# Row sort as two lanes of neighbours, bias rows on all partitions, sixteen image stores, new instruction orders

## The chip, the cores and the metric

The kernel runs on one core of a Trainium2 chip. The metric is the device time of one execution in microseconds (us), as the median of several runs. TensorE is called PE here, VectorE DVE, ScalarE ACT, GpSimd POOL and SyncE SP, as in the profile. All of the arithmetic is float32 but for one mask matmul.

## What is computed

Eight images of 32 x 32 tokens with 128 channels go through a deformable convolution, a correlation layer that sorts, windowed attention, a mixture of experts, a state-space layer and a second mixture of experts. What the change touches is this:

```python
om = conv3x3(xn, om_kernel) + om_bias            # offsets and masks
cols = bilinear gather of xn at (base + offset), times mask
x1 = x + cols.reshape(B, OH, OW, 9 * C) @ kernel + bias
...
x3 = x.reshape(b, m, c)                          # m = 1024 tokens
corr = jnp.einsum('bmc,bnc->bmn', x3, x3) / c
x_sort = jnp.sort(corr, axis=-1)[..., ::-1]
ranks = jnp.round(jnp.linspace(1.0, m - 1, 128)).astype(jnp.int32)
return x_sort[..., ranks]
```

So every one of the 1024 rows of an image's correlation matrix, 1024 values long, is sorted in descending order, and 128 of its ranks are kept.

## The kernel before

**Units.** An image is two units (halves h = 0 and 1) of 512 tokens. A unit's rows lie as four tiles: 128 partitions, each with 4 rows of 1024 values, so 4096 values in a partition. The stages of the program are F (group norm, deformable convolution and correlation of the next image), S (the sort, on DVE alone), C (attention, first experts, state-space layer) and M (second experts). They are software pipelined: while image i is sorted, F works on image i + 1, C on the halves (i - 1, 1) and (i, 0), and M on image i - 1.

**What sets the order.** Each engine runs its instructions in program order. The generators of the stages are woven by strings of letters in the table `ORDER` (`weave`, near the end of the file): a letter says from which stage the next piece comes. There is a string for each engine and each kind of image: fill (F of image 0 alone), early (image 0), full (images 1 to 6), late (image 7) and drain. Engines are tied by semaphores alone. POOL has the gathers of F and nothing else.

**The sort.** `pe_corr` makes the sum and the absolute difference of two halves of the columns, so that PE and ACT do the first compare-exchange (larger and smaller of each pair); ACT writes both to `corr` (L695) through `there`. `dve_S` does the rest with TENSOR_TENSOR max and min. Before, the row is 8 places of 128 values; a network that sorts 8 works across the places (`exchange`, L808 and L810, and L818 to L834), and its last layer scatters the results so that each run of 8 lies together: `Y` is a view of `corr` in which neighbours of an instruction's output are 8 values (32 bytes) apart. Then odd-even merges make runs of 16, 32, ... 512 (`compare` L794 and L796; `pairs` L873, L881, L901, L903; `eighth` L893; copies of the ends of runs L877 and L880), each down to distance k = 1. A bitonic merge of the two runs of 512 follows, of which the last steps (L927) make the wanted ranks alone. `corr` is free for the next unit (`corr_used`) after the compare of m = 16. Max and min of one step are two instructions; `link` is a semaphore that DVE counts for its own results.

**The image store.** `sp_F` writes the normalized image `xn_tok` four times, shifted, to `quads` in DRAM, so that one gather of 2 KB brings the four neighbours of a point: 8 token tiles x 4 corners = 32 stores of 64 KB an image, each with the outermost dimension ROWS = 4 in the destination. POOL gathers (`pool_F`) after all of the stores and after `idx` (L722), which DVE makes from the offsets. SP also issues the loads of the experts' weights (`e1w`, `e2w`), in the order that its strings give.

**Bias rows.** `conv_bias`, `bo_row` and `cb_row` lie on one partition and are added by a matmul with a row of ones (L605, L1053, L1296).

## Time and profile before

| | |
|---|---|
| median of 3 runs | 4914.16 us (4904.60 to 4914.23) |
| profiled execution | 4910.64 us, span 4908.8 us |
| DVE busy | 4267.6 us, 87% of the span |
| PE busy | 3958.7 us, 81% |
| ACT busy | 2954.4 us, 60% |
| POOL busy | 884.1 us, 18% |

The profile is of one execution. Its span goes from the first instruction to the last, and its own time is 1.8 us above the span. A busy share is a mean over fill, eight images and drain, which have different limits; a row of a group of instructions gives their count, summed busy time and the mean of one in ns, and behind the second bar the idle time of the engine just before them.

### The profile page before, as it was taken

What the parts mean: (1) busy time and instruction counts of PE and PEld (TensorE: products, weight loads), DVE (VectorE), ACT (ScalarE), POOL (GpSimd) and SP (SyncE); (2) the same over time, 40 slices, a digit from 0 to 9 for tenths busy, and PEclk for the clock granted to TensorE, in tenths of its full rate; (3) what the DMA queues carried; (4) which work ended last, traced back from release to release, by engine and by line L of the source; (5) the groups of instructions that cost most, each with busy time, mean ns of one, the idle gap of its engine ahead of it and who ended that gap; (6) DMA issues with size and microseconds to landing.
All of it is one profiled execution on the core that took longest, in us unless ns stands there. A gap on an engine that the chain in (4) does not pass through costs nothing.

```text
span 4908.8 us, 56286 instructions
## 1 busy us (share of the span) xinstructions
PE 3958.7 (81%) x19410; PEld 2667.5 (54%) x19410; DVE 4267.6 (87%) x5380; ACT 2954.4 (60%) x7241; POOL 884.1 (18%) x580
## 2 busy tenths in 40 slices
PE   5747748889798988989798988989798987867587
PEld 3616424567456654567456654567456654545354
DVE  1098999999999999999999999999999999999521
ACT  4526526687467846687467846677467845554452
POOL 2316000242005300242005300242005300000000
PEclk8878869999799998999799988999799998988798
DMA  4314100232013210232013210232013210010001
GB/s 132 98 35 123 37 0 18 67 105 63 16 43 110 79 36 18 71 104 65 11 43 110 79 36 18 71 102 63 14 44 110 77 34 16 20 30 27 10 24 37
DMA packets 226037, 269.28 MB, mean 55 GB/s; under 512 B 26831, under 2 KB 188506, under 8 KB 225626
## 3 DMA queue, kind: packets, MB, share of 16 engines
q0 software_dynamic: 46080, 151.03, 10.6%
q1 hardware_dynamic: 179674, 114.65, 8.0%
q8 instruction: 156, 2.56, 0.2%
q14 instruction: 127, 1.04, 0.1%
HBM read 242.25 MB, written 23.34 MB: 54 GB/s over the span
## 4 chain that ended last, share of the span: by engine, by line
DVE 41%; PE 36%; ACT 9%; issue 6%; POOL 4%; DMA 4%; SPq 1%; DVEq 0%; POOLq 0%; ACTq 0%
PE bank L597 5%; POOL gath L759 4%; PE bank L1298 3%; PE bank L1633 3%; PE bank L1628 3%; DMA gath<-quads,idx 3%; PE bank L1613 3%; DVE srt_b L794 3%; DVE srt_b L881 3%; DVE srt_b L796 3%; DVE srt_a L893 2%; DVE srt_b L873 2%; DVE srt_a L794 2%; DVE srt_a L796 2%; PE bank L569 2%
## 5 line engine op out<-in xcount | busy, mean ns | idle before, releaser
L759 POOL DMA_INDIRECT gath<-quads,idx x576 | 883.9, 1535 | 3075.4 <-DVE idx L722 1990.3
L597 PE MATMUL bank<-diag,gath 128*128 128x128 f32 x4608 | 615.0, 296 | 168.5 <-DMA gath<-quads,idx 168.5
L639 ACT ACTIVATE diag<-ident,w 128x128 f32<-128x128 f32 x2304 | 704.7, 393 | 30.7 <-DVE w L737 21.2
L597 PEld LDWEIGHTS bank<-diag,gath 128*128 128x128 f32 x4608 | 593.8, 211 | 203.9 <-DMA gath<-quads,idx 187.6
L1613 PEld LDWEIGHTS bank<-e2w,act 128*128 128x128 f32 (+1 forms) x3072 | 408.0, 198 | 161.3 <-issue 156.7
L1628 PE MATMUL bank<-mu_t,e2w 128*128 128x512 f32 (+1 forms) x768 | 421.9, 632 | 82.4 <-DMA e2w<-moe_w_t 36.2
L1633 PE MATMUL bank<-gated_u,e2w 128*128 128x512 f32 (+1 forms) x768 | 426.2, 638 | 36.7 <-DVE act L1713 32.9
L1713 DVE TENSOR_TENSOR act<-act,bank 128x512 f32<-128x512 f32 (+1 forms) x384 | 261.0, 680 | 183.6 <-PE bank L1633 160.8
L1613 PE MATMUL bank<-e2w,act 128*128 128x128 f32 (+1 forms) x3072 | 413.2, 281 | 1.6 <-DVE act L1713 1.6
L1681 ACT ACTIVATE act<-bank 128x512 f32<-128x512 f32 (+1 forms) x384 | 227.6, 593 | 208.6 <-PE bank L1628 206.0
L873 DVE TENSOR_TENSOR srt_b<-srt_a 128x1024 f32<-128x1024 f32 x192 | 350.9, 1828 | 1.5 <-issue 0.3
L881 DVE TENSOR_TENSOR srt_b<-srt_a 128x1024 f32<-128x1024 f32 x192 | 351.1, 1829 | 0.0
L1681 ACT ACT_TABLE_LOAD x199 | 255.3, 1283 | 3.4 <-PE bank L1613 0.4
L672 ACT ACTIVATE cols<-bank 128x384 f32<-128x384 f32 x192 | 93.0, 484 | 241.6 <-PE bank L597 235.8
L1633 PEld LDWEIGHTS bank<-gated_u,e2w 128*128 128x128 f32 (+1 forms) x768 | 131.3, 187 | 189.3 <-issue 166.6
L794 DVE TENSOR_TENSOR srt_b<-srt_a 128x2048 f32<-128x2048 f32 x96 | 219.3, 2285 | 1.4
L794 DVE TENSOR_TENSOR srt_a<-srt_b 128x2048 f32<-128x2048 f32 x96 | 219.2, 2283 | 0.9
L796 DVE TENSOR_TENSOR srt_b<-srt_a 128x2048 f32<-128x2048 f32 x96 | 219.2, 2283 | 0.0
L796 DVE TENSOR_TENSOR srt_a<-srt_b 128x2048 f32<-128x2048 f32 x96 | 219.1, 2283 | 0.0
L901 DVE TENSOR_TENSOR srt_a<-srt_b 128x2016 f32<-128x2016 f32 (+1 forms) x96 | 211.5, 2203 | 0.9
L903 DVE TENSOR_TENSOR srt_a<-srt_b 128x2016 f32<-128x2016 f32 (+1 forms) x96 | 211.6, 2204 | 0.0
L1628 PEld LDWEIGHTS bank<-mu_t,e2w 128*128 128x128 f32 (+1 forms) x768 | 121.3, 186 | 145.0 <-issue 73.5
(348 smaller groups left out, 8134.4 us busy)
## 6 DMA issues: line engine op xcount, KB each, us to landing
e2w<-moe_w_t SPq DMA_DIRECT2D x256, 170.5 KB
quads<-xn_tok SPq DMA_DIRECT2D x256, 64.0 KB
e1w<-L_ffn_w SPq DMA_DIRECT2D x256, 64.0 KB, 1.9
e2w<-moe_w_t SPq DMA_DIRECT2D x256, 64.0 KB
gath<-quads,idx POOLq DMA_INDIRECT x576
e2w<-moe_w_t SPq DMA_DIRECT2D x128, 42.5 KB
x_tok<-x SPq DMA_DIRECT2D x8, 512.0 KB, 4.4
out<-tm SPq DMA_DIRECT2D x16, 256.0 KB, 2.5
```

Source lines behind the costliest of these rows:

```text
L597: ins = T.matmul(FB[q % 2][:, k * P:(k + 1) * P], gath[:, g % 2, k, s * C:(s + 1) * C], diag[:, g % 2, 4 * k + s], start=(s == 0), stop=(s ...
L639: ins = SC.activation(diag[:, g % 2, n], ident[:], ACT.Copy, scale=w[:, n:n + 1])
L759: pool.indirect_dma_start(gath[:, g % 2, k], None, quads, bass.IndirectOffsetOnAxis(idx[:, TG * g + k:TG * g + k + 1], 0)).then_inc(sem["g ...
L794: V.tensor_tensor(dst[:, :, 0:size // 2], lo, hi, ALU.max)
L796: return V.tensor_tensor(dst[:, :, size // 2:size], lo, hi, ALU.min)
L873: V.tensor_tensor(out_lo, lo, hi, ALU.max)
L881: link.put(V.tensor_tensor(out_hi, lo, hi, ALU.min))
L1613: ins = T.matmul(MB[2][:, t * P:(t + 1) * P], act2[0:m, n % ACT2_SLOTS, t * P:(t + 1) * P], e2w[0:m, e % 2, W2 + k * C:W2 + (k + 1) * C], ...
L1628: T.matmul(MB[r % 2][0:m, :], e2w[:, e % 2, k * P:k * P + m], mu_t[:], start=True, stop=True).then_inc(sem["m_ps"], 1)
L1633: T.matmul(MB[r % 2][0:m, :], e2w[:, e % 2, W3 + k * P:W3 + k * P + m], gated_u[:], start=True, stop=True).then_inc(sem["m_ps"], 1)
L1681: SC.activation(act2[0:m, n % ACT2_SLOTS], MB[r % 2][0:m, :], ACT.Silu).then_inc(sem["m_sb"], 1)
L1713: V.tensor_tensor(act2[0:m, n % ACT2_SLOTS], act2[0:m, n % ACT2_SLOTS], MB[r % 2][0:m, :], ALU.mult).then_inc(sem["hh"], 1)
```

## The change

1. **Sort.** The pair that PE and ACT compare is now token j with token j + 512 (`sd` from the two contiguous halves of `yn_t`), and ACT writes the results in groups of four values: two larger, two smaller (`w=2`). A row is so two interleaved lanes of 512 values, and every later instruction moves at least two neighbours together. The network of 8 is gone. Odd-even merges run from m = 8 to m = 1024 and stop at distance k = 2, after which each lane is sorted. A new step compares lane 0 with lane 1 reversed and writes two halves apart (L876 and L878 of the new file), in place of the compare of size 1024. The rest of the bitonic merge is as it was. `corr` is only read, and is released after the first two instructions of a unit.
2. **Stores.** 16 stores of 128 KB take the place of 32 of 64 KB. Each takes 32 partitions of `xn_tok` with all eight tiles, and has the outermost dimension x = 32. They begin when both halves of `xn_tok` are there.
3. **Bias rows** are loaded to all 128 partitions and added by a matmul with the identity. In the preparation one DVE instruction and a wider matmul are added for it.
4. **Orders.** All strings but those of the fill and SP_early are new.

```diff
-        "CCCMMMCCCCCCCCMMFFMMMMMMMMCMCCCMCMMMF"
+        "CCCMMFFCMCCCCMCCCMMMMMMMMMCCCCMCMFMMM"
...
-        conv_bias = sb("conv_bias", [1, C])
+        conv_bias = sb("conv_bias", [P, C])
...
-            load(conv_bias[:], A["L0_conv_bias"].rearrange("a b c f -> (a b c) f"))
+            load(conv_bias[:], A["L0_conv_bias"].rearrange("a b c f -> (a b c f)").partition_broadcast(P))
...
+            V.tensor_scalar(tc[:, 1], ones[:], bqk[:, 2:3], None, ALU.mult)
...
-            T.matmul(CB[0][0:1, 0:C], bqk[:, 2:3], wqkvo[:, 3], start=True, stop=True).then_inc(prep, 1)
+            T.matmul(CB[0][:, 0:C], tc[:, 1], wqkvo[:, 3], start=True, stop=True).then_inc(prep, 1)
...
-            for t in range(NT):
-                if t % 4 == 0:
-                    sp.wait_ge(sem["xn_tok"], img("xn_tok", i, t // 4 + 1))
-                    settle(sp)
-                if t == 0:
-                    sp.wait_ge(sem["gath0"], img("gath0", i, 0))
-                    settle(sp)
-                    sp.wait_ge(sem["gath1"], img("gath1", i, 0))
-                    settle(sp)
-                for dy in range(2):
-                    for dx in range(2):
-                        there = q[ROWS * t + 1 - dy:ROWS * t + 1 - dy + ROWS, 1 - dx:1 - dx + WIDTH, 2 * dy + dx]
-                        sp.dma_start(there, xn_tok[:, t]).then_inc(sem["quad_out"], 16)
-                if t % 4 == 3:
-                    yield
+            sp.wait_ge(sem["xn_tok"], img("xn_tok", i, 2))
+            settle(sp)
+            sp.wait_ge(sem["gath0"], img("gath0", i, 0))
+            settle(sp)
+            sp.wait_ge(sem["gath1"], img("gath1", i, 0))
+            settle(sp)
+            for dy in range(2):
+                for dx in range(2):
+                    for r in range(ROWS):
+                        there = q[r + 1 - dy:r + 2 - dy + HEIGHT - ROWS:ROWS, 1 - dx:1 - dx + WIDTH, 2 * dy + dx]
+                        sp.dma_start(there.rearrange("t x c -> x t c"),
+                                     xn_tok[WIDTH * r:WIDTH * (r + 1)]).then_inc(sem["quad_out"], 16)
+                yield
...
-                    T.matmul(out, ones[0:1, :], conv_bias[:], start=False, stop=False)
+                    T.matmul(out, ident[:], conv_bias[:], start=False, stop=False)
...
-                there = corr[:, t % UT].rearrange("p (s k r) -> p s k r", k=2, r=P)
+                there = corr[:, t % UT].rearrange("p (b k w) -> p b k w", k=2, w=2)
...
-                    SC.activation(there[:, :, k], FB[1 - k][:].rearrange("p (s r) -> p s r", r=P), ACT.Identity,
+                    SC.activation(there[:, :, k], FB[1 - k][:].rearrange("p (b w) -> p b w", w=2), ACT.Identity,
...
-            pairs = yn_t[:].rearrange("p (s k r) -> p s k r", k=2, r=P)
-            V.tensor_tensor(sd[:, 1], pairs[:, :, 0], pairs[:, :, 1], ALU.subtract)
-            V.tensor_tensor(sd[:, 0], pairs[:, :, 0], pairs[:, :, 1], ALU.add).then_inc(sem["sd"], 1)
+            V.tensor_tensor(sd[:, 1], yn_t[:, 0:HALF], yn_t[:, HALF:TOK], ALU.subtract)
+            V.tensor_tensor(sd[:, 0], yn_t[:, 0:HALF], yn_t[:, HALF:TOK], ALU.add).then_inc(sem["sd"], 1)
...
-                if size == TOK:
-                    hi = hi[:, :, ::-1]
...
-            def places(buf):
-                return buf[:].rearrange("p g (s r) -> p g s r", s=8)
-
-            X, L, R, Y = places(corr), places(srt_a), places(srt_b), corr[:].rearrange("p g (r s) -> p g s r", s=8)
-
-            def exchange(lo, hi, out_lo, out_hi):
-
-                V.tensor_tensor(out_lo, lo, hi, ALU.max)
-                yield
-                link.put(V.tensor_tensor(out_hi, lo, hi, ALU.min))
-                yield
-                link.wait()
-
-            def fours(buf, b):
-                return buf.rearrange("p g (a b c) r -> p g a b (c r)", a=2, b=2)[:, :, :, b]
-
-            yield from exchange(fours(X, 0), fours(X, 1), fours(R, 0), fours(R, 1))
-            V.tensor_tensor(X[:, :, 1::4], R[:, :, 1::4], R[:, :, 2::4], ALU.max)
-            yield
-            link.put(V.tensor_tensor(X[:, :, 2::4], R[:, :, 1::4], R[:, :, 2::4], ALU.min))
-            yield
-            V.tensor_tensor(L[:, :, 3], R[:, :, 3], R[:, :, 7], ALU.max)
-            link.wait()
-            V.tensor_tensor(R[:, :, 1], X[:, :, 1], X[:, :, 5], ALU.max)
-            yield
-            V.tensor_tensor(L[:, :, 2], X[:, :, 2], X[:, :, 6], ALU.max)
-            V.tensor_tensor(L[:, :, 5], X[:, :, 1], X[:, :, 5], ALU.min)
-            yield
-            link.put(V.tensor_tensor(R[:, :, 6], X[:, :, 2], X[:, :, 6], ALU.min))
-            V.tensor_tensor(L[:, :, 4], R[:, :, 0], R[:, :, 4], ALU.min)
-            yield
-            link.wait()
-            V.tensor_tensor(Y[:, :, 0], R[:, :, 0], R[:, :, 4], ALU.max)
-            link.put(V.tensor_tensor(Y[:, :, 7], R[:, :, 3], R[:, :, 7], ALU.min))
-            yield
-            link.wait()
-            yield from exchange(L[:, :, 2:4], L[:, :, 4:6], R[:, :, 2:4], R[:, :, 4:6])
-            yield from exchange(R[:, :, 1:7:2], R[:, :, 2:7:2], Y[:, :, 1:7:2], Y[:, :, 2:7:2])
-            now = 1
-            m = 16
-            while m < TOK:
-                first = m == 16
-                if not first:
+            ins = yield from compare(8, runs(corr, 8), runs(srt_a, 8))
+            ins.then_inc(sem["corr_used"], 1)
+            yield
+            dve.wait_ge(sem["corr_used"], unit("corr_used", i, h))
+            now = 0
+            m = 8
+            while m <= TOK:
+                if m > 8:
                     link.wait()
-                ins = yield from compare(m, runs(corr if first else bufs[now], m), runs(bufs[1 - now], m))
-                if first:
-                    ins.then_inc(sem["corr_used"], 1)
-                else:
+                    ins = yield from compare(m, runs(bufs[now], m), runs(bufs[1 - now], m))
                     link.put(ins)
-                yield
-                if first:
-                    dve.wait_ge(sem["corr_used"], unit("corr_used", i, h))
-                now = 1 - now
+                    yield
+                    now = 1 - now
                 here, there = runs(bufs[now], m), runs(bufs[1 - now], m)
 
...
-                while k >= 1:
+                while k >= 2:
                     lo, hi = pairs(here, k)
                     out_lo, out_hi = pairs(there, k)
                     link.wait()
                     V.tensor_tensor(out_lo, lo, hi, ALU.max)
                     yield
-                    if k == 1:
-
-                        V.tensor_copy(edges(there, 0, 1), edges(here, 0, 1))
+                    if m == 8:
+
+                        link.put(V.tensor_tensor(hi, lo, hi, ALU.min))
+                        yield
+                        link.wait()
+                        link.put(V.tensor_copy(lo, out_lo))
+                        yield
+                        break
+                    if k == 2:
+
+                        V.tensor_copy(edges(there, 0, 2), edges(here, 0, 2))
                     elif k < m // 4:
 
                         V.tensor_copy(edges(there, 1, k // 2), edges(here, 1, k // 2))
                     link.put(V.tensor_tensor(out_hi, lo, hi, ALU.min))
                     yield
-                    if k == 1:
+                    if k == 2:
...
-            k = TOK
+            pair = bufs[now][:].rearrange("p g (j w) -> p g j w", w=2)
+            lo, hi = pair[:, :, :, 0], pair[:, :, ::-1, 1]
+            half = bufs[1 - now][:].rearrange("p g (w j) -> p g w j", w=2)
+            link.wait()
+            V.tensor_tensor(half[:, :, 0], lo, hi, ALU.max)
+            yield
+            link.put(V.tensor_tensor(half[:, :, 1], lo, hi, ALU.min))
+            yield
+            now = 1 - now
+            k = TOK // 2
```

Three places in the orders. On DVE, the start of the sort of image 1 (full), before; `srt_b` and `srt_a` are the sort's two buffers, the other rows belong to C and M:

```order
L808 TENSOR_TENSOR srt_b<-corr 128x8x256
L810 TENSOR_TENSOR srt_b<-corr 128x8x256
L1073 RECIPROCAL lnsd<-lnsd 128x4
L1074 SCALAR_TENSOR_TENSOR nmr<-lnmv,lnsd 128x4
L818 TENSOR_TENSOR corr<-srt_b 128x8x128
L820 TENSOR_TENSOR corr<-srt_b 128x8x128
L1152 TENSOR_REDUCE msm<-bank 128x4
L1153 TENSOR_TENSOR ml<-bank,msm 128x32
L822 TENSOR_TENSOR srt_a<-srt_b 128x4x128
L824 TENSOR_TENSOR srt_b<-corr 128x4x128
L826 TENSOR_TENSOR srt_a<-corr 128x4x128
L827 TENSOR_TENSOR srt_a<-corr 128x4x128
```

DVE at the same place now:

```order
L790 TENSOR_TENSOR srt_a<-corr 128x512x4
L792 TENSOR_TENSOR srt_a<-corr 128x512x4
L1046 RECIPROCAL lnsd<-lnsd 128x4
L1047 SCALAR_TENSOR_TENSOR nmr<-lnmv,lnsd 128x4
L829 TENSOR_TENSOR srt_b<-srt_a 128x512x2
L833 TENSOR_TENSOR srt_a<-srt_a 128x512x2
L836 COPY srt_a<-srt_b 128x512x2
L790 TENSOR_TENSOR srt_b<-srt_a 128x256x8
L792 TENSOR_TENSOR srt_b<-srt_a 128x256x8
L1125 TENSOR_REDUCE msm<-bank 128x4
L1126 TENSOR_TENSOR ml<-bank,msm 128x32
L829 TENSOR_TENSOR srt_a<-srt_b 128x256x4
```

The sixteen instructions of the 8-network begin here with two over 8 x 256 values, and in their place stand the compare of m = 8 and its one odd-even step with a copy; pieces are 4 or 2 values long every 8.

On SP, in the first full image, the loads of the second experts (`e2w`) and the stores of the next image, before:

```order
L1566 DMA e2w<-moe_w_t 128x341
L1568 DMA e2w<-moe_w_t 128x128 x2
L1568 DMA e2w<-moe_w_t 85x128
L502 DMA quads<-xn_tok 4x32x128 x32
L1565 DMA e2w<-moe_w_t 128x341
L1566 DMA e2w<-moe_w_t 128x341
L1568 DMA e2w<-moe_w_t 128x128 x2
L1568 DMA e2w<-moe_w_t 85x128
L1565 DMA e2w<-moe_w_t 128x341
```

SP at the stores of the same image now, with loads of the first experts (`e1w`) behind them:

```order
L1541 DMA e2w<-moe_w_t 85x128
L1538 DMA e2w<-moe_w_t 128x341
L1539 DMA e2w<-moe_w_t 128x341
L1541 DMA e2w<-moe_w_t 128x128 x2
L1541 DMA e2w<-moe_w_t 85x128
L501 DMA quads<-xn_tok 32x8x128 x16
L962 DMA e1w<-L_ffn_w 128x128
L963 DMA e1w<-L_ffn_w 128x128
L1538 DMA e2w<-moe_w_t 128x341
L1539 DMA e2w<-moe_w_t 128x341
L1541 DMA e2w<-moe_w_t 128x128 x2
L1541 DMA e2w<-moe_w_t 85x128
```

The stores now stand after the second set of `e2w` loads of the image, where before they followed the fifth, and eight pairs of `e1w` loads (lines 989 and 990 before, 962 and 963 now) that stood ahead of them stand behind.

On PE, in the same image, the transposes of the next image's normalized tokens, after which ACT makes `xn_tok`, before:

```order
L1633 MATMUL bank<-gated_u,e2w 128x512
L1312 MATMUL bank<-arena 128x128 x4
L1613 MATMUL bank<-e2w,act 128x128 x4
L1628 MATMUL bank<-mu_t,e2w 128x512
L1633 MATMUL bank<-gated_u,e2w 128x512
L1613 MATMUL bank<-e2w,act 128x128 x4
L561 MATMUL bank<-ident,yn_t 128x128 x4
L1628 MATMUL bank<-mu_t,e2w 85x512
L561 MATMUL bank<-ident,yn_t 128x128 x4
L1633 MATMUL bank<-gated_u,e2w 85x512
L1613 MATMUL bank<-e2w,act 128x128 x4
L1604 MATMUL bank<-gate_diag,mu 128x128 x4
```

PE at the transposes of the same image now (L952 and L1179 belong to the first experts of C):

```order
L1586 MATMUL bank<-e2w,act 128x128 x4
L1601 MATMUL bank<-mu_t,e2w 128x512
L1606 MATMUL bank<-gated_u,e2w 128x512
L1586 MATMUL bank<-e2w,act 128x128 x4
L1601 MATMUL bank<-mu_t,e2w 85x512
L560 MATMUL bank<-ident,yn_t 128x128 x8
L952 MATMUL bank<-ident,gates 8x128 x4
L1606 MATMUL bank<-gated_u,e2w 85x512
L1586 MATMUL bank<-e2w,act 128x128 x4
L1179 MATMUL bank<-u_t,e1w 128x512
L1183 MATMUL bank<-b,arena 128x128 x4
L1577 MATMUL bank<-gate_diag,mu 128x128 x4
```

The transposes (`bank<-ident,yn_t`) stand 59 rows earlier in PE's order, just ahead of the matmuls of a half's first experts (L1179), where before they followed a state-space layer's projections.

## Rows read from the trace of the kernel before

**Rows 1.** Page: busy us (share) xinstructions by engine; the chain by engine.

```profile
PE 3958.7 (81%) x19410; PEld 2667.5 (54%) x19410; DVE 4267.6 (87%) x5380; ACT 2954.4 (60%) x7241; POOL 884.1 (18%) x580
...
DVE 41%; PE 36%; ACT 9%; issue 6%; POOL 4%; DMA 4%; SPq 1%; DVEq 0%; POOLq 0%; ACTq 0%
```

**Rows 2.** Stretches: length, busy us and count by engine, PE clock, DMA share, GB/s.

```profile
0.00:247.70 247.70, 156.22 (x871) 121.63 (x871) 16.46 (x47) 118.92 (x356) 68.37 (x76) 0.88 0.39 114
...
2943.00:3496.00 553.00, 484.55 (x2427) 328.60 (x2426) 531.27 (x670) 369.53 (x907) 117.31 (x72) 0.92 0.20 60
...
4048.00:4586.00 538.00, 368.68 (x1554) 228.67 (x1554) 520.60 (x626) 260.51 (x556) 0.00 (x0) 0.84 0.07 21
4586.00:4908.80 322.80, 257.80 (x1126) 162.20 (x1126) 77.95 (x214) 161.86 (x346) 0.00 (x0) 0.89 0.09 27
```

**Rows 3.** Waits of DVE in one full image (2943 to 3496 us): us, times, longest.

```profile
DVE dtx L1476 <- ACT dtr L1404: 5.6, 2, 3.9
DVE act L1713 <- PE bank L1633: 4.4, 4, 2.2
DVE act L1713 <- ACT act L1681: 2.4, 2, 2.1
```

**Rows 4.** Groups by line and shape, DVE: count, busy us, mean ns, idle before.

```profile
L810 DVE TENSOR_TENSOR corr<-srt_b 128x1536 f32<-128x1536 f32 x16 | 47.1, 2942 | 0.0
...
L794 DVE TENSOR_TENSOR srt_a<-corr 128x2048 f32<-128x2048 f32 x16 | 36.5, 2284 | 0.0
...
L820 DVE TENSOR_TENSOR corr<-srt_b 128x1024 f32<-128x1024 f32 x16 | 19.5, 1218 | 0.0
...
L903 DVE TENSOR_TENSOR srt_a<-srt_b 128x2040 f32<-128x2040 f32 x16 | 36.4, 2276 | 0.0
...
L834 DVE TENSOR_TENSOR corr<-srt_b 128x512 f32<-128x512 f32 x16 | 17.6, 1099 | 0.0
...
L822 DVE TENSOR_TENSOR srt_a<-srt_b 128x512 f32<-128x512 f32 x16 | 10.9, 682 | 0.0
...
L877 DVE COPY srt_b<-srt_a 128x512 f32<-128x512 f32 x16 | 10.4, 648 | 0.0
L880 DVE COPY srt_a<-srt_b 128x256 f32<-128x256 f32 x32 | 9.3, 291 | 0.0
...
L880 DVE COPY srt_b<-srt_a 128x64 f32<-128x64 f32 x32 | 6.0, 189 | 0.0
```

**Rows 5.** DVE in order of time, first unit: start us, us of two instructions together.

```profile
275.15 1.29 DVE L893 TENSOR_TENSOR srt_a<-srt_a,srt_b 128x512 f32<-128x512 f32 x2
```

**Rows 6.** All engines in order of time, fill: start us, us, instruction.

```profile
34.94 22.66 SPq L502 DMA_DIRECT2D quads<-xn_tok  x32
...
55.49 0.23 DVE L722 SCALAR_TENSOR_TENSOR idx<-cols 128x72 uint32<-128x72 f32 x1
...
57.54 7.12 ACT L639 ACTIVATE diag<-ident,w 128x128 f32<-128x128 f32 x24 [4.04 <-DVE w L737]
62.10 1.08 POOL L759 DMA_INDIRECT gath<-quads,idx  x1 [61.66 <-DMA quads<-xn_tok]
...
68.51 3.79 PE L597 MATMUL bank<-diag,gath 128*128 128x128 f32 x16 [15.52 <-DMA gath<-quads,idx]
```

**Rows 7.** DMA while SP stores `quads`: the same columns as rows 2.

```profile
318.00:334.00 16.00, 13.36 (x38) 3.50 (x36) 15.86 (x10) 3.06 (x5) 0.00 (x0) 1.00 0.29 86
```

**Rows 8.** DMA view of 2310 to 2320 us, 40 slices: one store of `out` in it.

```profile
GB/s 0 0 0 0 0 0 0 0 0 0 0 0 0 0 0 59 293 287 295 115 0 0 0 0 0 0 33 0 0 0 0 0 0 0 0 0 0 0 0 0
```

**Rows 9.** Before the sort of image 2: start us, us; last `corr` written, first read.

```profile
1282.44 0.60 ACT L695 ACTIVATE corr<-bank 128x512 f32<-128x512 f32 x1 [1.12 <-PE bank L630]
...
1287.69 2.29 DVE L808 TENSOR_TENSOR srt_b<-corr 128x2048 f32<-128x2048 f32 x1
```

**Rows 10.** Groups by line and shape, PE: two matmuls of 320 columns.

```profile
L1298 PE MATMUL bank<-w_xbc,u_t 128*128 128x320 f32 x512 | 169.3, 478 | 0.0
...
L1296 PE MATMUL bank<-cb_row,ones 1*128 1x320 f32 x128 | 55.8, 517 | 0.0
```

More of the change, by code:

```diff
@@ L1052, in pe_att @@
             T.matmul(CB[0][:], ident[:], flat(u), start=False, stop=False)
-            T.matmul(CB[0][:], ones[0:1, :], row4(bo_row[:]), start=False, stop=False)
+            T.matmul(CB[0][:], ident[:], row4(bo_row[:]), start=False, stop=False)
             yield
@@ L1295, in pe_ssm @@
                 if conv:
-                    T.matmul(out[:, 0:XBC], ones[0:1, :], cb_row[:], start=True, stop=False)
+                    T.matmul(out[:, 0:XBC], ident[:], cb_row[:], start=True, stop=False)
                     for k in range(CONVK):
```

100 lines of the change are left out of this document (50 added, 50 removed).

## The prediction

> **What bounds the kernel now.** I read the page first: DVE is busy 87% of the span and leads the chain of work that ended last, with PE behind it [rows 1]. A mean hides the stages, so the table of stretches comes next [rows 2]. In the fill (to 247.7 us) DVE does nearly nothing and PE, ACT and the gathers set the time. In a full image, 2943 to 3496 us standing for six alike, DVE works 531.3 of 553.0 us, PE 484.6 and ACT 369.5. In the late image DVE works 520.6 of 538.0. Only in the drain, the last 322.8 us, is DVE idle again and PE the busiest. So from 247.7 to 4586 us the time is DVE's work plus some 22 us of idleness an image. The list of its waits shows many short ones on ACT and PE, the longest 3.9 us [rows 3]. What is taken from DVE's work here should come off the end almost whole; what is taken from PE or ACT should not.
>
> **The sort, per unit.** Contiguous max and min fit a line: 512 values 682 ns, 1024 values 1218, 2048 values 2284 [rows 4], so 1.043 ns a value and 148 ns fixed. Two of 512 stand in 1.29 us together [rows 5], so each starts 0.08 us before the other is recorded as done and the fixed part on the path is about 0.07 us. Removed are the network, 16 instructions over 15360 values (4096 + 2048 + 3072 + 1024 + 2048 + 3072), and the six steps of distance 1 in m = 16 to 512, 12 instructions over 2 x 11784 = 23568 values. Added are m = 8, 4 instructions over 6144 values, and m = 1024, 22 instructions over 32784. Both sums are 38928 values: the comparisons are the same, in 26 instructions instead of 28, which is 0.14 us. The gain lies elsewhere. The last network layer writes single values 32 bytes apart: 1536 values in 2942 ns, where the line gives 1750, and 512 values in 1099 ns, where contiguous ones take 682 [rows 4]. Two of each are 2 x 1.19 + 2 x 0.42 = 3.2 us, and all of it goes. Copies cost something back. Three copies of ends at distance 1 go: 0.65 us for the 512 values of m = 16, and by its rate and the shorter rows 0.29 and 0.19 for 128 and 32. New are 1024 values in pairs, and ends of 256, 64 and 16. Copies in pieces give 291 ns for 256 and 189 for 64 [rows 4], 0.53 ns a value: 0.70 us for 1024, and 0.66 for the three. That is 1.36 against 1.13, a loss of 0.23. Net 3.2 + 0.14 - 0.23 = 3.1 us a unit, **50 us in 16 units**.
>
> Patterns that are new have these bounds. The pieces of 4 and 2 values every 8 (7168 values a unit): nearest is the step on eighths of a run at m = 16, pieces of 8 bytes every 64, two in 1.29 us with nothing on top [rows 5]; the far end is the 0.8 ns a value of the scattered write. I take nothing, since the pieces are alike. The merge across lanes reads every second value, one side backwards: the distance-1 step over 2040 values reads and writes every second one in 2276 ns, on the line [rows 4], so I take nothing. The copy of 1024 could go at the rate of 648 ns for 512 single values, 0.4 us a unit or 6 us in all more. The rows show that single values every 32 bytes pay and every 8 bytes don't. The Trainium skill, SBUF — State Buffer, section on the DMA port swizzle, says that accesses run at full bandwidth when at least two in a row hit the same 16-byte line. By that rule all new patterns are free, on ACT's side too, and the sum stays; by the far end it would be the slower rival below.
>
> ACT writes `corr` in pieces of 8 bytes every 16 instead of blocks. The eviction takes 0.60 us [rows 9], eight of them for a half; even doubled they add 4.8 us to a chain that ACT, with 180 us free an image, otherwise bears.
>
> **The corr chain** is the cover to watch. The last `corr` of image 2 is written at 1282.44 + 0.60 = 1283.0 us and DVE first reads it at 1287.7 [rows 9]: 4.7 us of cover. DVE gains 6.2 us an image, so with F where it was, DVE would wait 1.5 us at each of seven image starts, 10 us in all. In the new order the transposes stand 59 rows earlier on PE, and `corr` is released after two instructions instead of after the compare of m = 16, so I take nothing and keep the 10 us for the range.
>
> **Stores.** In the fill SP issues 32 stores from 34.94 us for 22.66 us, and POOL's first gather waits for them until 62.10 [rows 6]. While they run, the DMA engines are busy to 0.29 and move 86 GB/s [rows 7], where the store of `out`, outermost dimension 128, reaches 290 GB/s with shares of 9 tenths [rows 8]. So a store with outermost dimension 4 uses about 4 of 16 engines. With 32 outermost, 2 MB would take 7.2 us at 290 GB/s; at the old issue time of 22.66 / 32 = 0.71 us each, 16 take 11.3. From 35 us on they have landed by 51 us even with the 4.5 us of the old tail. The gathers also need `idx`, which DVE writes at 55.49 + 0.23 us [rows 6]; so POOL starts near 55.9, 6.2 us sooner, and not 15. ACT's first weights (from 57.54, 12 in 3.6 us) and PE's first gather matmul (68.51) follow at 61 to 62.5 us. Against this stand one DVE instruction in the preparation and 288 KB of broadcast loads, 1.0 us at 290 GB/s if nothing hides them: 0.8 us. The fill gives **5.4 us**. In later images the stores lie beside DVE's sort and give SP 10 us or more.
>
> A rule speaks against the new stores. The Trainium skill, SBUF — State Buffer, section on the DMA port swizzle, says that 32 partitions reach only 8 of 16 ports, 189 GB/s as measured there. By it the stores would take 11 us instead of 7; `idx` still comes later, so the sum stays.
>
> **Bias rows.** The matmul with one row of ones over 320 columns takes 517 ns, that with 128 rows 478 [rows 10]. The rows don't set the time, and PE is not the bound: nothing.
>
> **Orders.** They move waits and no work. DVE's 22 us an image are spread over many short waits [rows 3], and what the new strings make of them no row can show. Bounds: a better order could halve them, 7 x 10 = 70 us less; a worse one adds as much. I take no change, because PE keeps 68 us free an image [rows 2].
>
> **Sum.** 4908.8 - 50 - 5.4 = 4853.4 us of span, 4855.2 with the 1.8 us around it. The profiled execution (4910.64) is 3.5 us under the median of the runs, which I leave out: **4855 us**, 1.2% less.
>
> **Rivals.**
> - Better orders: DVE's waits fall by 10 us in most images, 4855 - 60 = 4795. For it: the longest waits are 2 to 4 us in the image shown, and sit on few places. Against: the order before already left few. 15%.
> - Waits grow: DVE is faster, PE and ACT are not, and the chains that release DVE come late, by the 1.5 us above or up to 4 us an image. 4865 to 4900, say 4882. 22%.
> - The change doesn't gain: 50 us of new waits eat the sort's gain, 4905 to 4923. PE's 68 us free would have to lie in the wrong places. 4%.
> - Slower: pieces of 4 and 2 values every 8 pay like single ones. 7168 x 0.78 ns = 5.6 us a unit, 89 us in 16, so 4944. It decides from 3.1 us / 7168 = 0.43 ns a value. The eighths at m = 16 speak against it [rows 5]. 4%.
> - Slower by SP: the stores stand three `e2w` sets and eight `e1w` pairs earlier, and SP holds everything behind them until both halves of `xn_tok` are there. If PE reaches the transposes late, experts' weights come late, and PE, then DVE, wait. It decides from the point at which PE's 68 us are used up; 15 us an image more would give 4855 + 105 = 4960. The transposes moved along on PE, which speaks against it. 5%.
>
> **Chances.** My forecast (4840 to 4865) 50%, the rest as above. The range leaves out the two slower cases, the one without gain and the tip of the better orders: 4795 to 4897 us. A measurement of this kernel can tell about 0.2% (10 us) from no change. Faster by more 0.87, within it 0.04, slower 0.09.
>
> **What would show it.** DVE's busy time down by about 50 us with 15 fewer instructions; the first two instructions of a unit at 2284 ns and the step at m = 8 at 1218; the copy of 1024 near 700 ns; the sort's lane merge at 2284. The stretch of a full image near 547 us with 22 us idle. In the fill, 16 stores over 7 to 11 us with a DMA share well over 0.3, POOL's first gather at 56 us waiting for `idx`, and the first sort at 242 us. A wait for `corr` at the start of a unit would show the cover gone; a wait of PE for `e1w` or `e2w` the SP rival. A new eviction time over 0.6 us on ACT would show that its pieces cost.

## The result and the profile after

| | before | changed |
|---|---|---|
| median | 4910.75 us (4904.6 to 4914.23) | **4749.86 us** (4744.98 to 4753.61) |
| profiled execution | 4910.64 us, span 4908.8 | 4753.48 us, span 4751.4 |
| mean granted TensorE clock, of 2.4 GHz | 0.896 | 0.909 |

The ratio is 0.9676, with a 95% interval of 0.9664 to 0.9688. The change takes off 161 us, 3.3%. The forecast was 55 us, and the time lies 45 us below its range.

The page of the changed kernel, to be held against [rows 1]: busy time by engine, and the shares of the chain that ended last.

```profile
PE 3878.9 (82%) x19410; PEld 2642.8 (56%) x19410; DVE 4219.8 (89%) x5365; ACT 3009.5 (63%) x7284; POOL 928.2 (20%) x580
...
DVE 74%; PE 15%; issue 6%; ACT 3%; DMA 1%; SPq 1%; POOL 0%; DVEq 0%; POOLq 0%; ACTq 0%
```

DVE's busy time is 48 us less. PE's is 80 us less with the same 19410 instructions, which the forecast didn't foresee. The chain now runs over DVE for 74% of the span instead of 41%, and over PE for 15% instead of 36%.

Stretches of the changed kernel: length, busy us by engine (PE, PEld, DVE, ACT, POOL), PE clock, DMA share, GB/s. They are the fill, the first image, a full image, the late image and the drain.

```profile
0.00:241.30 241.30, 153.69 (x870) 120.35 (x870) 16.73 (x47) 119.52 (x356) 68.39 (x76) 0.88 0.42 118
241.30:710.10 468.80, 280.77 (x1305) 198.95 (x1306) 460.38 (x475) 198.84 (x551) 125.19 (x72) 0.78 0.18 51
...
2840.20:3371.50 531.30, 466.46 (x2427) 318.93 (x2426) 524.96 (x670) 376.97 (x913) 122.37 (x72) 0.95 0.21 62
3905.10:4426.90 521.80, 375.85 (x1554) 235.31 (x1552) 514.27 (x619) 262.92 (x557) 0.00 (x0) 0.84 0.07 22
4426.90:4751.40 324.50, 259.78 (x1126) 166.91 (x1126) 78.46 (x214) 167.00 (x350) 0.00 (x0) 0.86 0.09 27
```

By stage the time went as follows (first unit's sort to first unit's sort; full images are the mean of six):

| us | before | changed | less |
|---|---|---|---|
| fill | 247.7 | 241.3 | 6.4 |
| first image | 489.1 | 468.8 | 20.3 |
| a full image | 551.9 | 532.5 | 19.4, and 117 in six |
| late image | 537.9 | 521.9 | 16.0 |
| drain | 322.5 | 324.4 | -1.9 |

In a full image DVE's work fell from 531.3 us [rows 2] to 525.0 in the row shown, the 6.2 us of the forecast. The other 13 us are idle time: DVE had 20 to 22 us of it an image, and has 6 to 8.5 now. That is the term that was missed. The waits of DVE over all stages with a sort show it (us in total, times, longest). First the kernel before:

```profile
DVE dtx L1476 <- ACT dtr L1404: 34.9, 15, 3.9
DVE act L1713 <- PE bank L1633: 30.0, 19, 4.9
...
DVE lnsd L1073 <- ACT lnsd L1063: 14.6, 1, 14.6
DVE arena L1539 <- PE bank L1361: 12.4, 9, 1.5
DVE act L1713 <- ACT act L1681: 11.2, 12, 2.1
```

and the changed one:

```profile
DVE arena L1512 <- PE bank L1334: 8.6, 8, 1.7
DVE lnsd L1046 <- issue: 3.2, 1, 3.2
DVE act L1686 <- PE bank L1606: 1.3, 2, 0.9
```

The 35 us for `dtr`, the 41 for `act` and 11 of the 15 for `lnsd` are gone or all but gone. What is left idle in an image is mostly the spacing between instructions.

### The profile page after: what moved, and what is told of

It reads as the page before. It is cut to its first block, busy times and chain, and to the rows that moved or that the text cites. A ratio compares the mean times of both kernels' runs of the same rounds, so it can differ in the third digit from the quotient of the medians.

```text
span 4751.4 us, 56186 instructions
## 1 busy us (share of the span) xinstructions
PE 3878.9 (82%) x19410; PEld 2642.8 (56%) x19410; DVE 4219.8 (89%) x5365; ACT 3009.5 (63%) x7284; POOL 928.2 (20%) x580
## 3 DMA queue, kind: packets, MB, share of 16 engines
q14 instruction: 125, 1.02, 0.1%
## 4 chain that ended last, share of the span: by engine, by line
DVE 74%; PE 15%; issue 6%; ACT 3%; DMA 1%; SPq 1%; POOL 0%; DVEq 0%; POOLq 0%; ACTq 0%
DVE srt_b L845 6%; DVE srt_b L829 6%; DVE srt_a L792 5%; DVE srt_a L790 5%; DVE srt_a L857 4%; DVE srt_b L792 4%; DVE act L1686 4%; DVE srt_a L867 4%; DVE srt_a L845 4%; DVE srt_b L790 4%; DVE srt_a L865 3%; DVE srt_b L857 3%; DVE srt_a L829 3%; PE bank L596 2%; DVE srt_b L865 2%
## 5 line engine op out<-in xcount | busy, mean ns | idle before, releaser
L757 POOL DMA_INDIRECT gath<-quads,idx x576 | 928.0, 1611 | 2844.1 <-DVE idx L721 1861.2
L596 PE MATMUL bank<-diag,gath 128*128 128x128 f32 x4608 | 598.1, 291 | 134.4 <-DMA gath<-quads,idx 127.2
L596 PEld LDWEIGHTS bank<-diag,gath 128*128 128x128 f32 x4608 | 579.7, 206 | 173.6 <-DMA gath<-quads,idx 145.6
L1606 PE MATMUL bank<-gated_u,e2w 128*128 128x512 f32 (+1 forms) x768 | 440.2, 657 | 97.6 <-DVE act L1686 72.8
L1586 PEld LDWEIGHTS bank<-e2w,act 128*128 128x128 f32 (+1 forms) x3072 | 424.2, 204 | 165.4 <-issue 162.7
L1586 PE MATMUL bank<-e2w,act 128*128 128x128 f32 (+1 forms) x3072 | 428.8, 288 | 0.8 <-DVE act L1686 0.6
L829 DVE TENSOR_TENSOR srt_b<-srt_a 128x1024 f32<-128x1024 f32 (+3 forms) x208 | 370.1, 1779 | 2.3 <-issue 0.2
L845 DVE TENSOR_TENSOR srt_b<-srt_a 128x1024 f32<-128x1024 f32 x192 | 350.6, 1826 | 0.0
L790 DVE TENSOR_TENSOR srt_a<-srt_b 128x2048 f32<-128x2048 f32 x112 | 255.8, 2284 | 0.8
L792 DVE TENSOR_TENSOR srt_a<-srt_b 128x2048 f32<-128x2048 f32 x112 | 255.8, 2284 | 0.0
L792 DVE TENSOR_TENSOR srt_b<-srt_a 128x2048 f32<-128x2048 f32 x96 | 219.3, 2284 | 0.0
L829 DVE TENSOR_TENSOR srt_a<-srt_b 128x1024 f32<-128x1024 f32 (+2 forms) x112 | 194.3, 1735 | 1.5
```

Source lines behind the costliest of these rows:

```text
L596: ins = T.matmul(FB[q % 2][:, k * P:(k + 1) * P], gath[:, g % 2, k, s * C:(s + 1) * C], diag[:, g % 2, 4 * k + s], start=(s == 0), stop=(s ...
L757: pool.indirect_dma_start(gath[:, g % 2, k], None, quads, bass.IndirectOffsetOnAxis(idx[:, TG * g + k:TG * g + k + 1], 0)).then_inc(sem["g ...
L790: V.tensor_tensor(dst[:, :, 0:size // 2], lo, hi, ALU.max)
L792: return V.tensor_tensor(dst[:, :, size // 2:size], lo, hi, ALU.min)
L829: V.tensor_tensor(out_lo, lo, hi, ALU.max)
L845: link.put(V.tensor_tensor(out_hi, lo, hi, ALU.min))
```

## Experiments: the parts one by one

First the parts were tried apart. Orders were exchanged over the new sort alone; the new orders without the new sort weren't tried. The edits are the hunks of the change, put in or left out:

```
sort    dve_S, sd and corr as changed; orders, stores and bias rows as before
stores  sp_F with 16 stores (quad_out 16 * 16); the rest as before
bias    conv_bias, bo_row, cb_row on [P, ...], ident[:] in place of ones[0:1, :]
orders  the ORDER table of the one kernel or of the other
```

> The kernel before with the new sort and its layout of corr alone; old strings, stores and bias rows. Theory 1: 16 x 3.1 = 50 us less, 4860 us. Theory 2 in its corr half: waits fall too, 4780 or lower. A third reading (DVE 6 us an image faster runs into chains that PE and ACT set): 4870 to 4890, with a wait for corr at the start of units.

> The kernel before with the 16 new stores alone. Theory 1: the fill 6 us shorter and nothing else, 4905 us. Theory 2 in its store half (expert loads that stood behind 22 us of stores were what PE and then DVE waited for): 10 us or more less in each of 7 images, 4840 or lower.

> The changed kernel with every order string of the kernel before; sort, stores and bias rows are new. Theory 1 (the new strings alone took DVE's waits of 14 us an image): 4855 us, DVE busy as in the changed kernel (4220), idle 22 us in a full image. Theory 2 (the early release of corr and the faster stores freed the chains that DVE waited for, whatever the strings): 4750 to 4780, idle about 8 us in a full image.

> The changed kernel with the 32 old stores, which now stand early in SP's strings. Theory 1: the fill 6 us longer, 4756 us. If the new strings lean on short stores (loads of e1w and e2w stand right behind them): waits of PE for e2w or e1w in each full image and 4775 to 4850 us.

These four left some 50 us without an owner: the sort alone took off 0.59%, the stores 0.18%, yet sort, stores and bias rows together 1.77%. So the bias rows, forecast at nothing, came under suspicion, and five more kernels completed the picture.

> The kernel before with the bias rows on 128 partitions and nothing else of the change. Theory A (the bias rows hold TensorE for 56 us): 4850 to 4885 us, and TensorE busy 473 us in a full image where 482 stood. Theory B (TensorE has slack of 60 us an image, so nothing shows): 4900 to 4910 us. In both the spacing at the bias rows falls to 1.30, 0.56 and 1.51 us.

> The kernel before with the new sort and correlation layout and the bias rows on 128 partitions; old orders, old 32 stores. The sort alone gave 4879, sort, bias rows and new stores together 4820. Theory A (bias rows): 4825 to 4840 us, with VectorE's idle time in a full image down from 20 to 26 us to 14 to 18. Theory B (what is missing comes from the sort and the short stores together): 4870 to 4880 us.

> The kernel before with the new sort and the 16 new stores; old orders, bias rows on one partition. Theory A (bias rows): the sum of sort and stores, 4865 to 4875 us. Theory B (sort and short stores together make up what neither gives alone): 4820 to 4830 us.

> The changed kernel with the bias rows back on one partition (rows of one partition against a row of ones), all else as changed. Theory A (the bias rows): in the traces the first output step after a one-partition bias matmul starts late, 1.69 us from the product before the conv bias row to the second product behind it against 1.30 us with the full-height bias, 0.94 against 0.56 at the 3x3 bias, 1.90 against 1.51 at the attention bias: 0.39 us each, 64 + 64 + 16 of them in the program, 56 us of TensorE's time, of which the chains that VectorE waits for take most. It expects 4785 to 4810 us, TensorE busy 476 us or more in a full image (468 in the changed kernel) and VectorE's idle time in one at 10 to 14 us instead of 7. Theory B (the orders alone hold the gain beyond the sort): 4745 to 4760 us and VectorE's idle time unchanged. Theory C (the new orders fit only the changed work): 4810 us or more, as with the old stores.

> The kernel before with the new sort and correlation layout and the new orders; old 32 stores, bias rows on one partition. The last corner of the cube of orders, stores and bias rows over the new sort. With the old orders it took 4879 us. If the parts add under the new orders (bias rows 32 us, stores 64 us over the changed kernel's 4750) it takes 4840 to 4855 us. If the new orders bring a gain of their own and both lacks fall into the same waits, 4815 to 4835 us. If the new orders need the other parts, 4870 us or more.

Measured, as ratios to the kernel before run beside them, with their 95% intervals:

| new parts | old orders | new orders |
|---|---|---|
| stores alone | 0.9982 (0.9972 to 0.9991), 4897.7 us | |
| bias alone | 0.9919 (0.9902 to 0.9935), 4863.0 us | |
| sort | 0.9941 (0.9925 to 0.9958), 4879.5 us | 0.9909 (0.9891 to 0.9927), 4853.5 us |
| sort, stores | 0.9945 (0.9929 to 0.9962), 4875.6 us | 0.9746 (0.9727 to 0.9766), 4781.8 us |
| sort, bias | 0.9839 (0.9822 to 0.9855), 4824.5 us | 0.9807 (0.9791 to 0.9824), 4814.2 us |
| sort, bias, stores | 0.9823 (0.9807 to 0.984), 4820.3 us | 0.9676 (0.9664 to 0.9688), 4749.9 us |

From one set of runs to the next the median of the kernel before moved between 4901 and 4911 us, so the ratios are compared; 0.01% is 0.49 us. The four runs of sort and stores under the new orders spread most, 4775 to 4800 us.

Of the first four expectations, the one for the sort alone was met in its third range (4870 to 4890), but with no wait for `corr` beyond the first sort's. The stores alone fell between their two theories (4897.7 us, and 3.5 us of the fill instead of 6), and so did the old orders (4820.3 us). The old stores met the second, with a wait for `e1w` in each full image. Of the next five, the bias rows alone lie in the range of theory A and the other three within 3.5 us of it, far from B; sort and orders alone lie where the parts add. Three things follow.

The **sort** alone is worth 29 us, over half of the 50 us that leave DVE: its idle time in a full image grew to 20 to 26 us. The **bias rows** are worth 40 us alone and, over the sort, 50 to 60 with the old orders and 34 to 50 with the new. The **orders** are worth 16 us as long as the old stores stand, with or without bias rows, and 72 to 98 us with the short ones. The stores in turn gave 9 us at most under the old orders, and 64 to 80 under the new. Orders and stores are one term, not two.

What the new orders take away is seen in the kernel that differs from the changed one in its orders alone, by DVE's waits over the same stages:

```profile
DVE act L1686 <- PE bank L1606: 26.6, 19, 3.9
...
DVE lnsd L1046 <- issue: 14.9, 1, 14.9
...
DVE dtx L1449 <- ACT dtr L1377: 9.8, 8, 2.5
DVE act L1686 <- ACT act L1654: 6.8, 5, 2.1
DVE msm L1125 <- PE bank L1558: 6.3, 4, 1.7
```

These are 64 us, of which 4.5 are left in the changed kernel, and its full images take 540.9 us instead of 532.5. Which of the strings does it was not tried: but for the last two stages they were exchanged all at once. The granted clock in a full image is also a little higher with them, 0.94 to 0.95 against 0.93 to 0.94, and whether that is a cause of the shorter time or follows from it, no run separates. Beside the bias rows it is no rival: with them alone it stayed at 0.93 to 0.94, where the kernel before had 0.92 to 0.93.

## Experiments: what the bias rows cost

The rows of PE's weight loads in order of time tell it, in the kernel before (start us, us, instruction; in brackets the idle time ahead and its cause):

```profile
2511.13 0.46 PEld L1300 LDWEIGHTS bank<-w_zdt,u_t 128*128 128x128 f32 x2
2511.93 0.29 PEld L1296 LDWEIGHTS bank<-cb_row,ones 1*128 1x128 f32 x2 [0.34 <-issue]
2512.66 1.91 PEld L1298 LDWEIGHTS bank<-w_xbc,u_t 128*128 128x128 f32 x8 [0.44 <-issue]
```

The load of the one-partition weights starts 0.34 us after the load ahead of it has ended, and the full one behind it 0.44 us after. Neither waits for a semaphore ("issue"). In the changed kernel such rows show no gap worth a bracket (medians 0.03 and 0.08 us):

```profile
2437.49 0.41 PEld L1269 LDWEIGHTS bank<-cb_row,ident 128*128 128x128 f32 x2
2437.99 2.07 PEld L1271 LDWEIGHTS bank<-w_xbc,u_t 128*128 128x128 f32 x8
```

The gaps are not the loss itself: at this place the two grow by 0.67 us together, and PE loses 0.39. That is read from start to start on PE, where each float32 product stands as two instructions. Around `cb_row` the five steps are 0.316, 0.374, 0.358, 0.373 and 0.269 us with the old row, and 0.222 and four times 0.269 with the new one: each of four steps is about 0.1 us longer. From the start of the instruction ahead of the bias row's two to the start of the third behind them:

| us | one partition | 128 partitions |
|---|---|---|
| `cb_row`, 64 times | 1.689 | 1.299 |
| `conv_bias`, 64 times | 0.943 | 0.558 |
| `bo_row`, 16 times | 1.898 | 1.508 |

These are medians, the same to 1 ns in four kernels with old rows and four with new ones. It is 0.39 us each time, 144 times, so **56 us of PE**. The means that the forecast compared, 517 and 478 ns [rows 10], hold a fifth of that (0.04 us for each of the two instructions), since the rest lies in the gaps and in the products behind.

Why DVE's time follows is seen in the kernel with the bias rows alone. Its waits of DVE, as above:

```profile
DVE act L1714 <- PE bank L1634: 31.9, 24, 5.0
DVE srt_b L809 <- ACT corr L696: 23.5, 1, 23.5
DVE lnsd L1074 <- issue: 21.0, 1, 21.0
DVE arena L1540 <- PE bank L1362: 10.6, 9, 1.7
DVE msm L1153 <- PE bank L1586: 10.1, 6, 2.1
DVE dtx L1477 <- ACT dtr L1405: 6.2, 8, 1.2
DVE act L1714 <- ACT act L1682: 3.2, 4, 1.4
```

DVE's wait for `dtr` falls from 34.9 us to 6.2, and that for ACT's part of `act` from 11.2 to 3.2: 37 us, of which 6 come back at `lnsd` and 4 at `msm`. `dtr` is made by ACT from the four products with `w_zdt`, and on PE these alternate with the convs that `cb_row` opens, so three convs stand ahead of the last. PE as a whole had 68 us free in an image, but at this place DVE was waiting. (The 24 us for `corr` are the first sort's wait, in every kernel.)

How low may the rows be? One kernel gave the bias matmuls of the changed kernel other heights:

```
-T.matmul(out[:, 0:XBC], ident[:], cb_row[:], ...
+T.matmul(out[:, 0:XBC], ident[0:64, :], cb_row[0:64], ...
...
-T.matmul(out, ident[:], conv_bias[:], ...
+T.matmul(out, ident[0:32, :], conv_bias[0:32], ...
...
-T.matmul(CB[0][:], ident[:], row4(bo_row[:]), ...
+T.matmul(CB[0][:], ident[0:96, :], row4(bo_row[:])[0:96], ...
```

> The changed kernel with each bias matmul on fewer partitions: the conv bias row on 64, the 3x3 bias on 32, the attention bias on 96 (the bias then reaches only that many rows of its tile, so this part of the computation is left out for the others). Read is the spacing of the products around each bias matmul. Theory A (any height under 128 breaks the overlap of weight load and product): 1.69, 0.94 and 1.90 us at all three, as with one partition, and about 4780 us. Theory B (only the narrowest rows do): 1.30, 0.56 and 1.51 us, and 4745 to 4755 us.

The spacing was 1.691 us at 64 partitions, 0.943 at 32 and 1.512 at 96, the time 4762.1 us (ratio 0.972, 0.9699 to 0.974). So both theories failed in part: 64 and 32 rows cost as much as one, 96 cost nothing. The kernel lost 12 us by its median and 22 by the ratio, less than the 32 to 34 of the kernel with all three rows on one partition, though 128 of the 144 places are as slow; that isn't explained. (It is two runs here, and four there that spread over 25 us.)

The matmuls of the second experts (L1586) narrow the step further. Some stand on 85 partitions among full ones, and their starts lie 0.112 us apart on both sides, as those of full ones do; one over 32 partitions behind them starts at 0.205 us. So the step lies between 64 and 85 partitions.

The Trainium skill has the rule behind this: TensorEngine Tiling (Array Packing), section Tiling Modes, lists 128, 64 and 32 rows as modes of the array and says that "Changing tiling mode (not just tile) drains the TensorE". The rows agree in where the step lies: 1, 32 and 64 partitions fit a smaller mode and pay, 85 and 96 need the full one and don't. That it is a drain, no row shows. Counted over PE's records, neighbours pass between at most 64 partitions and more 480 times in the kernel before and 192 times in the changed one; the edit takes away 144 changes there and back. Those left are at products over 8, 27 and 32 partitions. At 0.39 us there and back they would hold 37 us of PE, by an estimate; whether DVE waits for any of it, no run tells.

## Experiments: what the long stores cost under the new orders

With the 32 old stores under the new orders, DVE's largest wait and PE's wait for a load were, over all stages with a sort (us, times, longest):

```profile
DVE act L1688 <- PE bank L1608: 67.2, 14, 11.3
```

```profile
PE bank L1181 <- DMA e1w<-L_ffn_w: 52.2, 6, 9.2
```

PE waits once an image for a load of `e1w`, 9 us, and DVE as long for a product behind it; the changed kernel has 1.3 us of the one and none of the other. Nine of the ten us that a full image is longer (542.7 to 532.5) are these. SP's order in a full image is why: it stands in `CCCMMFFCM` at the stores (`FF`), waits 95 us for `xn_tok`, issues the stores, and only then the load of `e1w` that PE needs next. In the changed kernel the stores take 8.6 us, that load goes out at 2919.4, 9.4 us after the first store, and PE starts on it at 2927.4 without a wait. With the old stores it goes out 22.6 us after the first store, at 2972.7, and PE starts on it at 2976.8 after 8.6 us of idleness. The rival of the forecast had this mechanism; it was right about the place and wrong that the new kernel would suffer from it, because the stores got shorter.

To tell it from the traffic of the stores, they were moved six places down the string, behind five pairs of `e1w` and one set of `e2w` (the expectation counts one pair fewer, and its 128-byte rows are rows of 128 values):

```
-"CCCMMFFCMCCCCMCCCMMMM...
+"CCCMMCMCCCCFFMCCCMMMM...
```

> The changed kernel with the 32 old stores (4814 us), but in a full image with the stores five loads later in SyncE's order, behind four pairs of e1w and one load of e2w, which then no longer stand behind 22 us of stores. Theory A (the 10 us an image are the loads of e1w queued behind the stores: the profile has TensorE waiting 8.6 us once an image for e1w and VectorE 9.7 us for the product behind it): 4750 to 4775 us, and that wait is gone. Theory B (the traffic of the 128-byte-row stores itself or the later gather costs): 4805 us or more.

4824.3 us (0.9844, 0.9826 to 0.9861): nothing won, and in the range of theory B. Theory A seemed to fall, but the wait had moved. PE over all stages with a sort:

```profile
PE bank L1603 <- DMA e2w<-moe_w_t: 76.5, 15, 10.5
```

The wait for `e1w` is gone, and in its place PE waits 76.5 us for `e2w`, whose load now stands behind the stores; with the stores at the earlier place it was 14.8 us in 9 waits, 3.3 at most. DVE's wait for the product behind is 73.8 us. So the two halves of the stores went where no load behind them was due:

```
-"CCCMMFFCMCCCCMCCCMMMM...
+"CCCMMCMCCCCFMCCCFMMMM...
```

> The changed kernel with the 32 old stores (4814 us), in a full image in two halves of 11 us at two places of SyncE's order where no load behind them is due: one before the e2w load that goes out 11 us after the last paced pair of e1w, one behind the three unpaced pairs of e1w, where the next e2w load stood 16 us off. Theory A (what the long stores cost is the one load behind them that TensorE is next to want, whichever it is): 4755 to 4780 us, with no wait of TensorE for e1w or e2w over 3 us in a full image and VectorE's idle time there at 6 to 10 us. Theory B (long stores cost by their traffic or by the later gathers wherever they stand): 4805 to 4830 us, as in the two places tried.

**4751.5 us** (0.9676, 0.9653 to 0.9698) with the 32 old stores, the changed kernel's time. Full images take 531 to 533.5 us. What was 67.2 us of waiting is now:

```profile
DVE act L1688 <- PE bank L1608: 1.6, 2, 1.2
```

PE's waits for `e2w` are back at 15.4 us, 3.2 at most, against 15.7 and 3.5 in the changed kernel. Theory A holds, and the time is 3.5 us below its range: the cost was the one load next in line. So in full images the 16 stores bring nothing that a better place for the 32 doesn't. What they bring by themselves is 3.6 us of the fill (244.9 and 241.3 us).

## Experiments: the price of DVE's time, and the last stages

To price DVE's time, work of no use was added behind the sort's first two instructions:

```
...
+            V.tensor_reduce(more[:, 0:CONVK], w_xbc[:], AX.X, ALU.max)
+            V.tensor_reduce(more[:, CONVK:CONVK + TAPS], conv_w[:], AX.X, ALU.max)
...
```

> The changed kernel with two maxima over constants added behind the sort's first stage, 2432 elements in two instructions; by the 1153 ns of such an instruction over 960 elements that is 2.9 us a unit, 47 us in 16 units, their result unused. It prices VectorE's time under the new orders. Theory A (VectorE sets the time one to one, as the prediction had it): 4790 to 4800 us. Theory B (part of it fills idle time, 7 us an image): 4765 to 4785 us. Theory C (every us lengthens other waits too): over 4805 us.

The added instructions (busy us in all, mean ns):

```profile
L802 DVE TENSOR_REDUCE more<-w_xbc 128x4 f32<-128x1280 f32 x16 | 23.6, 1475 | 0.0
...
L803 DVE TENSOR_REDUCE more<-conv_w 128x9 f32<-128x1152 f32 x16 | 21.5, 1343 | 0.0
```

45.1 us of DVE's work cost 33 us by the medians, 4782.7 us (0.976, 0.9742 to 0.9777) against 4749.9, and 41 by the ratios. So a us of DVE's work is worth 0.7 to 0.9 us under the new orders, and by that estimate the sort's 50 us some 36 to 46; under the old orders they were 29 alone and 39 over the bias rows. The time is in the range of theory B, but idle time took up little: in a full image it went from 7.5 to 6.7 us on the mean. DVE's busy time grew by 41.4 us, less than the durations, since each instruction starts before the one ahead is recorded as done.

> The changed kernel with the orders of the last stage alone as before (four strings). The last stage took 324.4 us in the changed kernel and 313 to 320 us in kernels with old orders. If that is the strings of that stage, 4738 to 4746 us, below the changed kernel; if it hangs on what the stage before leaves over, 4748 to 4756 us.

> The changed kernel with the orders of the last full stage and of the drain as before (eight strings). By the stages of the kernel with all old orders (530.2 and 320.1 us against 521.9 and 324.4): 4752 to 4756 us, if what the new orders bring comes stage by stage and not from how stages meet; over 4765 us in the other case.

> The changed kernel with the four old strings of the last stage, beside the changed kernel itself on one chip. By the stage's 3.7 us (320.7 against 324.4 in the profiles) 3 to 5 us less than the changed kernel beside it.

> The changed kernel, for the kernel with the old orders of the last stage to be held against: 4745 to 4753 us.

The drain took 324.4 us in the changed kernel and 320.7 with its old strings: 4746.4 us (0.966, 0.964 to 0.9681). With the late image's old strings too it was 4747.2 us, the late image at 527.0 instead of 521.9 and the drain at 316.6. Beside one another on one chip, the kernel with the old drain had 4744.1 us (4737.8 to 4752.5) and the changed one 4746.9 (4743.5 to 4748.6). Three us are within the spread, so no version here beats the changed kernel for certain. What the runs show is that the new strings bring nothing in the last two stages together; their gain lies in the full images (8.4 us each, 540.9 to 532.5) and the first (12.6 us, 481.4 to 468.8). For the late image's strings both theories had expected more than the 4747.2 us (4752 and up), and the pair on one chip lie 2.7 us apart, just under the 3 to 5 expected.

## Why the prediction was wrong

**What bounds the kernel.** Right: DVE. Its busy time per full image fell by 6.3 us, to 525.0, where 6.2 were said, and the kernel stayed bound by it. Wrong was the sentence that "what is taken from PE or ACT should not" come off the end. A us from PE at a place where DVE waits did.

**Sort.** The work is right to the us. DVE has 15 fewer instructions, and the durations of all of them sum to 4545.0 us against 4595.0. The first unit in order of time (start us, us):

```profile
241.32 2.29 DVE L790 TENSOR_TENSOR srt_a<-corr 128x2048 f32<-128x2048 f32 x1 [24.19 <-ACT corr L694]
243.53 2.28 DVE L792 TENSOR_TENSOR srt_a<-corr 128x2048 f32<-128x2048 f32 x1
245.85 1.23 DVE L829 TENSOR_TENSOR srt_b<-srt_a 128x1024 f32<-128x1024 f32 x1
247.00 1.22 DVE L833 TENSOR_TENSOR srt_a<-srt_a 128x1024 f32<-128x1024 f32 x1
248.25 0.70 DVE L836 COPY srt_a<-srt_b 128x1024 f32<-128x1024 f32 x1
```

The first two at 2.29 and 2.28 us, m = 8 at 1.23 and 1.22, the copy of 1024 at 0.70: each on the value taken. The merge across lanes takes 2288 and 2284 ns, so pieces of 8 bytes and every second value cost nothing, and the slower rival is out. The Trainium skill (SBUF — State Buffer, section on the DMA port swizzle) lets two hits on a 16-byte line keep the rate, and these rows of DVE agree. On ACT's side, which the forecast took in, they don't quite: its eviction in pieces of 8 bytes went from 595 to 637 ns, where it was to stay at 0.60. No wait of DVE shows for it. That the 50 us come off "almost whole" was right for the new kernel within 0.7 to 0.9, and wrong under the old orders.

**The corr chain.** Taken as nothing, and it is: DVE waits for `corr` only ahead of the first sort (24.2 us, in the row above; 23 before).

**Fill.** 6.4 us against 5.4, but by other terms. The stores of the fill, two stretches of 8.6 us beside such stores later, and the fill's `idx`, first gather and first weights for it:

```profile
36.24 8.53 SPq L501 DMA_DIRECT2D quads<-xn_tok  x16
```

```profile
281.70:290.30 8.60, 8.60 (x19) 2.00 (x18) 8.53 (x11) 0.00 (x0) 0.00 (x0) 0.85 0.84 205
2910.00:2918.60 8.60, 8.60 (x40) 4.61 (x39) 8.60 (x5) 2.97 (x5) 0.00 (x0) 1.00 0.84 204
```

```profile
56.83 0.23 DVE L721 SCALAR_TENSOR_TENSOR idx<-cols 128x72 uint32<-128x72 f32 x1
...
58.18 1.08 POOL L757 DMA_INDIRECT gath<-quads,idx  x1 [57.73 <-issue]
...
64.34 7.73 PEld L596 LDWEIGHTS bank<-diag,gath 128*128 128x128 f32 x48 [10.11 <-DMA gath<-quads,idx]
```

SP issues the 16 stores in 8.5 us, in the 7 to 11 expected, and the DMA share beside them is 0.84 where it was 0.29 [rows 7], so at least 14 of the 16 engines carry them. The packets of those in the fill run from 37.1 to 46.5 us, 2.10 MB at 223 GB/s; the 204 and 205 of the stretches take in the start, when none runs. The Trainium skill, SBUF — State Buffer, section on the DMA port swizzle, has 189 GB/s as measured for 32 partitions; what was measured here is 18% above that and well below the 290 that the forecast took for its 7.2 us. It has no effect on the sum. `idx` came at 56.8 instead of 55.5 and the gather 1.3 us behind it, 3.9 us sooner than before instead of 6.2. By themselves the stores take 3.5 us off the fill (244.2 us with them alone) and the bias rows 3.2 (244.5 us).

**Bias rows: "nothing".** The first step that failed. It was priced by mean durations, which leave out most of what the narrow matmul costs from start to start, and then put at nothing because "PE is not the bound". The runs gave 56 us of PE, and by the ratios 34 to 60 us of time, as DVE's waits for `dtr` and `act` shrank with it.

**Orders: "no change".** The second, and the larger. The bounds were 70 us either way and the middle was taken because PE had 68 us free; measured are 72 us less with the short stores (0.9823 to 0.9676). What was free on PE over a whole image said nothing of the waits of DVE at `act`, `lnsd`, `dtr` and `msm`, 64 us with the old strings and 4.5 with the new. The range took in a better order or the sort's gain, but not 50 us of bias rows on top of both. The rival "Better orders" (4795) named the mechanism and had 15%. The rival by SP had the mechanism of the old stores, 10 us a full image.

In the sum: forecast 50 + 5.4 + 0 + 0 = 55. Measured along one path, from the ratios: sort 29, bias rows 50, stores 8, orders 72, together 159 us (0.59, 1.02, 0.16 and 1.47%). In another sequence the shares differ, as the table shows; the sum doesn't.

## What to carry over

Price an edit on an engine that has time to spare by the waits of the bound engine on its chain, and not by its share of busy time: 68 us free an image did not hide 0.39 us on the chain that DVE waits for. Read a matmul's cost from start to start, up to the products behind it, since the mean duration leaves out the gaps. A long run of DMA issues costs what the one load behind it is late, so its place among the loads on that queue matters as much as its length; and when one such place is tried and the time stays, look whether the wait has only moved.

## What was not expected of the hardware

- A matmul whose operands stand on 1, 32 or 64 partitions among full-height ones makes four steps from start to start about 0.1 us longer each, 0.39 us in all. At 96 partitions there was none of it (1.512 against 1.508 us), nor at 85 (0.112 us between starts on both sides).
- ACT's eviction of 512 values in pieces of 8 bytes took 637 ns against 595 in blocks, while DVE's reads and writes in such pieces stayed at 2284 ns for 2048 values.
- Stores from 32 partitions with an outermost dimension of 32 kept the 16 DMA engines busy to 0.84 at 204 to 205 GB/s (223 from first packet to last); stores with an outermost dimension of 4 kept them busy to 0.29 at 86 [rows 7].
